# First attention: the values of all nine key tiles of a third of the queries in one group, exponentials in 18 slots, tail keys padded to 128 rows

## The reference, cut to what matters

```python
# _L0_attn_ref: x is (8 images, 1056 tokens, 64), 8 heads of 8 columns
attn = jnp.einsum('bnhd,bmhd->bhnm', q * scale, k)
attn = jax.nn.softmax(attn + bias[None], axis=-1)      # bias depends on n - m
out = jnp.einsum('bhnm,bmhd->bnhd', attn, v).reshape(Bw, Nw, Cd)
```

## Time and profile before

| | |
|---|---|
| median of 3 runs | 2691.78 us (2688.55 to 2697.84) |
| the profiled execution | 2689.29 us, its span 2687.5 us |
| the first attention | from about 335 to 1223 us of the span |
| busy share of the whole span | PE 91%, DVE 71%, ACT 53%, POOL 15% |
| mean granted TensorE clock | 0.91 |

### The profile page before, as it was taken

The page is one execution under the profiler, slowest core; times in us unless marked ns, Lnnn a source line. Parts: engine busy times, 40 slices in busy tenths (PEclk is TensorE's granted clock), DMA queues, the critical chain, the costliest instruction groups (busy, mean ns, idle before and its releaser), DMA issues. The chain is left out here.

```text
span 2687.5 us, 51435 instructions
## 1 busy us (share of the span) xinstructions
PE 2455.1 (91%) x18136; PEld 1069.5 (40%) x18136; DVE 1911.8 (71%) x4910; ACT 1437.0 (53%) x2468; POOL 394.1 (15%) x489
## 2 busy tenths in 40 slices
PE   8987689999999999997799997987799998799999
PEld 3336523333333333335333333666544444433333
DVE  4566688889888889873577776659677774366665
ACT  2117637777777777772344443427666765144333
POOL 2002100000000000005111112132101002311110
PEclk9997779999999999996899999666699999599999
DMA  2114511101010101306100000245612241600110
GB/s 92 24 32 155 194 30 27 37 26 37 25 37 25 37 25 37 61 9 130 28 21 22 22 22 22 65 106 159 226 45 84 64 98 43 138 16 17 32 25 12
DMA packets 233520, 155.14 MB, mean 58 GB/s; under 512 B 187617, under 2 KB 192546, under 8 KB 233042
## 3 DMA queue, kind: packets, MB, share of 16 engines
q1 hardware_dynamic: 220098, 123.57, 17.2%
q0 software_dynamic: 10368, 19.06, 2.5%
q10 hardware_dynamic: 2808, 9.22, 1.5%
HBM read 86.75 MB, written 65.09 MB: 57 GB/s over the span
## 5 line engine op out<-in xcount | busy, mean ns | idle before, releaser
L1666 DVE TENSOR_REDUCE att_mpart<-ps 128x1 f32<-128x512 f32 x1024 | 633.7, 683 | 55.7 <-PE ps L1486 50.6
L1624 ACT ACTIVATE att_p<-ps 128x704 f32<-128x704 f32 x768 | 546.5, 760 | 214.8 <-PE ps L1551 207.8
L1580 PE MATMUL ps<-att_p,att_v 128*9 128x352 f32 x3072 | 300.7, 462 | 0.1
L1486 PE MATMUL ps<-att_kT,att_qT 64*128 64x512 bf16 x1024 | 281.2, 386 | 20.9 <-DMA att_qz<-qt_d 8.4
L1551 PE MATMUL ps<-att_qT,att_kT 64*128 64x352 bf16 x1536 | 251.5, 317 | 7.3 <-ACT att_p L1624 6.9
L1280 DVE TENSOR_REDUCE cau_mpart<-ps 128x1 f32<-128x512 f32 (+5 forms) x384 | 193.1, 552 | 81.1 <-PE ps L1106 61.1
L2418 ACT ACTIVATE mo_act<-ps,mo_b 128x768 f32<-128x768 f32 x176 | 156.3, 901 | 132.0 <-PE ps L2300 127.4
L2571 DVE TENSOR_TENSOR mo_g<-mo_act,ps 128x768 f32<-128x768 f32 x176 | 167.4, 951 | 77.3 <-PE ps L2335 41.2
L1247 ACT ACTIVATE cau_p<-ps 128x704 f32<-128x704 f32 (+6 forms) x272 | 171.6, 660 | 82.3 <-PE ps L1165 49.7
L2970 ACT ACTIVATE mo_act<-ps 128x1024 f32<-128x1024 f32 (+1 forms) x108 | 102.9, 953 | 195.9 <-PE ps L2884 195.6
L1551 PEld LDWEIGHTS ps<-att_qT,att_kT 64*128 64x128 bf16 x1536 | 82.0, 93 | 272.9 <-issue 263.2
(11 more groups left out here) (419 smaller groups left out, 3928.9 us busy)
## 6 DMA issues: line engine op xcount, KB each, us to landing
qt_d<-pre_qT SPq DMA_DIRECT2D x8, 1056.0 KB, 4.3
kt_d<-pre_kT SPq DMA_DIRECT2D x8, 1056.0 KB, 7.3
att_kT<-kt_d SPq DMA_DIRECT2D x32, 264.0 KB, 2.8
att_qT<-qt_d SPq DMA_DIRECT2D x32, 264.0 KB, 3.0
cqt_d<-cpr_qT SPq DMA_DIRECT2D x8, 1056.0 KB
cau_qT<-cqt_d SPq DMA_DIRECT2D x16, 528.0 KB, 4.1
o_d<-att_o POOLq DMA_DIRECT2D x128, 37.1 KB, 2.7
cv_d<-cpr_v POOLq DMA_DIRECT2D x16, 288.0 KB, 6.0
```

What stands on the lines that cost most here:

```text
L1486: mm = pe.matmul(ps[:, bank, :], qT[half(s), u, j * P:(j + 1) * P], kT[half(s), u, c * BANK:(c + 1) * BANK], start=True, stop=not near)
L1580: mm = pe.matmul(ps[32 * cg:32 * cg + DV, 7, 0:TH], v[:, u, i, s, :], p[:, r, s, :], start=i < 2, stop=i == FULL - 1)
L1624: e = act.activation(p[:, n % PRING, :, :], ps[:, bank:bank + 2, 0:TH], ACT.Exp)
L1666: red = dve.tensor_reduce(mpart[:, j, s, c:c + 1], ps[:, bank, :], AX.X, ALU.max)
```

## The change

The nine units of a third become one group, so a third has one `scores` of nine units and one `values` of sixteen matmuls plus two for the tail. `PRING` goes from 4 to 18, two thirds of exponentials. The tail's two value matmuls contract over 128 rows and not 64: `vt` gets 128 rows and POOL sets the lower 64 of `vt` and of the two tail slots of `p` to zero once. In the list of maxima one of the three tail-query maxima moves to index 21, and the order of the last four changes, so that the side steps right ahead of the tail's scores in thirds 0 and 1 are tail-query maxima. The number of side steps behind each unit is a written tuple (`sides`), 13 a third; those of the tail unit come ahead of its scores and not behind. On ACT a finished third is copied out behind the first exponential of the group after the next. Semaphore targets are counted through the whole stage.

```diff
-    QT, MRING, PRING = 2, 3, 4
+    QT, MRING, PRING = 2, 3, 18
...
-    groups = [(t, [(t, i) for i in part]) for t in range(3) for part in ((0, 1), (2, 3), (4, 5), (6, 7), (None,))]
+    groups = [(t, [(t, i) for i in part]) for t in range(3) for part in ((*range(FULL), None),)]
...
-    third_last = [5 * t + 4 for t in range(3)]
+    third_last = list(range(3))
...
-    maxes += [("keys", s, 0, 0) for s in range(2)] + [("query", 0, 0, c) for c in range(3)]
+    maxes.insert(21, ("query", 0, 0, 0))
+    maxes += [("query", 0, 0, c) for c in range(1, 3)] + [("keys", s, 0, 0) for s in range(2)]
...
-    cut = [len(side) * c // NU for c in range(NU + 1)]
+    sides = (2, 1, 2, 1, 1, 2, 1, 1, 2) * 2 + (2, 1, 1, 3, 1, 1, 1, 1, 2)
+    cut = [sum(sides[:c]) for c in range(NU + 1)]
...
-        vt = nm.sb("vt", [64, U, 2, DV])
+        vt = nm.sb("vt", [P, U, 2, DV])
...
+            pool.wait_ge(mz_set, 1)
+            pool.memset(vt[2 * TT:P, :, :, :], 0.0).then_inc(blank, 1)
+            pool.wait_ge(blank, 1)
+            for i in range(2):
+                pool.memset(p[2 * TT:P, NT * i + FULL, :, :], 0.0).then_inc(blank, 1)
+                pool.wait_ge(blank, 2 + i)
...
+                    if i is None:
+                        for pos in range(cut[unit], cut[unit + 1]):
+                            side_step(it, u, pos, last)
+                    at_least(pe, p_made, n - 1)
...
-                    for pos in range(cut[first_unit[g] + c], cut[first_unit[g] + c + 1]):
-                        side_step(it, u, pos, last)
+                    if i is not None:
+                        for pos in range(cut[unit], cut[unit + 1]):
+                            side_step(it, u, pos, last)
...
                     if i is None:
-                        apart(pe, const)
+                        pe.wait_ge(blank, 3)
                     for s in range(2):
                         if i is None:
-                            mm = pe.matmul(ps[64 * s:64 * s + DV, 7, 0:TH], vt[:, u, s, :], p[0:2 * TT, r, 0, :], start=False,
+                            mm = pe.matmul(ps[64 * s:64 * s + DV, 7, 0:TH], vt[:, u, s, :], p[:, r, 0, :], start=False,
                                            stop=True)
...
+                            if c == 0 and len(pending) == 2:
+                                out_third(*pending.pop(0))
+                        pending.append((it, u, t))
```

More of the change, by code:

```diff
@@ L1334, in attend_heads @@
     place = [(m - AHEAD if m >= AHEAD else side.index(("max", 2, m))) % MRING for m in range(NM)]
-    cut = [len(side) * c // NU for c in range(NU + 1)]
+    sides = (2, 1, 2, 1, 1, 2, 1, 1, 2) * 2 + (2, 1, 1, 3, 1, 1, 1, 1, 2)
+    cut = [sum(sides[:c]) for c in range(NU + 1)]
+    assert cut[NU] == len(side) and side[cut[9] - 1][2] == 21 and side[cut[18] - 1][2] == 34
     with ExitStack() as ctx:
@@ L1355, in attend_heads @@
         cdel = nm.sb("cdel", [P, 3, 160 * 8])
-        (set_up, mz_set, mrow_set, t_in, cor_rest, cor_hi, s_mm, p_made, pv_mm, o_cp, mx_mm, mx_red, m_row, m_hi, m_r1, m_mid,
+        (set_up, blank, mz_set, mrow_set, t_in, cor_rest, cor_hi, s_mm, p_made, pv_mm, o_cp, mx_mm, mx_red, m_row, m_hi, m_r1, m_mid,
          c_made, t_mm, t_cp) = nm.sems(
-            "set_up", "mz_set", "mrow_set", "t_in", "cor_rest", "cor_hi", "s_mm", "p_made", "pv_mm", "o_cp", "mx_mm", "mx_red", "m_row",
+            "set_up", "blank", "mz_set", "mrow_set", "t_in", "cor_rest", "cor_hi", "s_mm", "p_made", "pv_mm", "o_cp", "mx_mm", "mx_red", "m_row",
             "m_hi", "m_r1", "m_mid", "c_made", "t_mm", "t_cp")
@@ L1388, in load @@
                              (v[:, u, :, :, :], v_d[bi].rearrange("b p (u t s d) -> (b p) u t s d", u=U, t=NT, s=2)[:, u, :, :, :]),
-                             (vt[:, u, :, :], vt_d[bi].rearrange("b p (h d) -> (b p) h d", d=DV)[:, 2 * u:2 * u + 2, :])):
+                             (vt[0:2 * TT, u, :, :], vt_d[bi].rearrange("b p (h d) -> (b p) h d", d=DV)[:, 2 * u:2 * u + 2, :])):
                 sp.dma_start(dst, src).then_inc(loads[u], 16)
@@ L1541, in scores @@
                 for c, (_, i) in enumerate(parts):
-                    n = u * NU + first_unit[g] + c
-                    pe.wait_ge(p_made, it * U * NU + n - 1 if n >= 2 else it * U * NU)
+                    unit = first_unit[g] + c
+                    n = (it * U + u) * NU + unit
+                    if i is None:
+                        for pos in range(cut[unit], cut[unit + 1]):
+                            side_step(it, u, pos, last)
+                    at_least(pe, p_made, n - 1)
                     apart(pe, const)
@@ L1559, in scores @@
                     mm.then_inc(s_mm, 1)
[L1560 to L1561 removed]
+                    if i is not None:
+                        for pos in range(cut[unit], cut[unit + 1]):
+                            side_step(it, u, pos, last)
             def values(it, u, g):
                 t, parts = groups[g]
[L1566 to L1568 removed]
+                n0 = (it * U + u) * NU + first_unit[g]
+                at_least(pe, o_cp, (it * U + u) * 3 + t)
                 for c, (_, i) in enumerate(parts):
[L1570 removed]
+                    pe.wait_ge(p_made, n0 + c + 1)
                     r = (n0 + c) % PRING
                     if i is None:
[L1573 removed]
+                        pe.wait_ge(blank, 3)
                     for s in range(2):
                         if i is None:
[L1576 removed]
+                            mm = pe.matmul(ps[64 * s:64 * s + DV, 7, 0:TH], vt[:, u, s, :], p[:, r, 0, :], start=False,
                                            stop=True)
@@ L1582, in values, with start @@
                 mm.then_inc(pv_mm, 1)
[L1584 to L1597, removed]
+            def start(k):
+                pe.wait_ge(t_cp, (k + 1) * QT)
+                scores(k // U, k % U, 0, k >= pairs - U)
+            start(0)
+            for k in range(pairs):
+                for g in range(NG):
+                    if g + 1 < NG:
+                        scores(k // U, k % U, g + 1, k >= pairs - U)
+                    elif k + 1 < pairs:
+                        start(k + 1)
+                    values(k // U, k % U, g)
         @block.scalar
@@ L1601, in _, with out_third, step @@
             enter(act, const, "act")
[L1602 to L1609, removed]
+            def out_third(it, u, t):
+                act.wait_ge(pv_mm, (it * U + u) * NG + third_last[t] + 1)
+                if t == 0:
+                    at_least(act, stored[u % 2], (it * (U // 2) + u // 2) * 64)
+                act.activation(o[:, u % 2, t * TH:(t + 1) * TH], ps[:, 7, 0:TH], ACT.Identity).then_inc(o_cp, 1)
+            def step(it, pending):
                 for u in range(U):
@@ L1612, in step @@
                         for c, (_, i) in enumerate(parts):
[L1613 to L1619, removed]
+                            n = (it * U + u) * NU + first_unit[g] + c
+                            act.wait_ge(s_mm, n + 1)
+                            old = n - PRING
+                            if old >= 0:
+                                act.wait_ge(pv_mm, (old // NU) * NG + group_of[old % NU] + 1)
                             bank = 2 * (n % 2)
@@ L1625, in step @@
                             e.then_inc(p_made, 1)
[L1626 to L1633, removed]
+                            if c == 0 and len(pending) == 2:
+                                out_third(*pending.pop(0))
+                        pending.append((it, u, t))
+            pending = []
+            for it in range(IT):
+                step(it, pending)
+            for left in pending:
+                out_third(*left)
         @block.vector
```

## The result

| | before | after |
|---|---|---|
| median | 2690.62 us (2688.55 to 2697.84, 4 runs) | 2965.95 us (2963.68 to 2976.54, 4 runs) |
| ratio after / before | | 1.103 (1.099 to 1.106) |
| the profiled execution, its span | 2689.29 us, 2687.5 us | 2976.54 us, 2974.7 us |
| mean granted TensorE clock of the span | 0.91 | 0.85 |
| one pair of heads, mean over 31 | 26.79 us | 35.05 us |

The kernel is 10% slower. The prediction had 2866 us, with 2930 as the upper end: right in direction, 100 us short. The profiled execution of the changed kernel is the slowest of its four, 10.6 us above their median.

What follows compares the result with a forecast made beforehand. PE was taken to set the pace with 2% to spare, DVE close behind at 11%. Longer pairs (+168), the last pair (+5) and the start (+4) made +177 us on 2689.3: 2866 us, range 2800 to 2930.

Steps and rivals of the forecast that it cites:

- DVE runs dry at the values run: During eighteen value matmuls PE makes no maximum; DVE, with three banks (1.8 us) stored, would idle 2.4 us.
- terms of 6.80 and 3.06: In a third: PE starts side step 13 at 6.80 us, released by DVE; the values run lasts 3.06 us.
- The sum of a pair: First, middle and last third of a pair take 10.6, 10.3 and 11.4 us: 32.3 against 26.8, +5.5.
- 168 forecast: The added 5.5 us a pair, holding for about 30.5 pairs of the stage: +168 us.
- The clock falls: Rival: PE, used less in the DVE-paced phase, drops its clock; 2.9 us more a third, about 3130 us; chance 0.07.
- The other argument: Against a clock fall: where the clock was seen to fall, PE did nothing at all (1660.4 to 1663.8).
- The last pair: Last pair of the stage, paced by ACT: 8.8 us a third against 7.06, +1.7 three times, +5 us.
- The start: At the stage's start the first values come a third later, with the clock lower until then: +4 us.
- The profile I said to look for: In the stage's windows PE's busy share falls to some 80 to 85%, DVE's to about 74%, ACT's to about 60%.
- The sign named as "wrong": Sign against the forecast: a clock under 0.95 in the stage, putting the time above the range.
- 3.4 us a pair of PE's turns: PE's saving from one values group a third instead of five: about 1.1 us a third, 3.4 a pair.

Runs made afterwards that it cites:

- run 4: Changed kernel with each full-maximum reduction on DVE reading 256 of 512 columns, leaving half the keys out of the maxima; 2772.17 us.
- run 5: Changed kernel with full tiles' score matmuls issued twice and full-maximum reductions reading 256 of 512 columns; 2806.33 us.
- run 8: Changed kernel with a third's nine tiles in two groups (0 to 3; 4 to 7 and the tail) instead of one; 2820.80 us.
- run 9: Changed kernel with a third's tiles in four groups, pairs of tiles, the tail with the last pair; 2707.74 us.
- run 10: Kernel of run 9 with a finished third copied out behind the exponentials of the very next group; 2685.86 us.
- run 1: Changed kernel with each full tile's two score matmuls issued twice into the same place (second copies, redundant work); 2885.36 us.
- run 2: Changed kernel with score matmuls issued twice for even key tiles only; 2883.41 us.
- run 3: Changed kernel with score matmuls issued twice for every fourth key tile only; 2900.22 us.
- run 13: Changed kernel with the tail's two value matmuls contracting over 64 rows again, with the turn before them; 2997.96 us.
- run 6: Changed kernel with a third's last three side steps moved behind the first eight value matmuls of the run ahead of it; 2930.59 us.
- run 7: Kernel of run 6 with full tiles' score matmuls also issued twice; 2873.78 us.

## Why the prediction was right or wrong

- **DVE runs dry at the values run: right.** Step 13 at 6.79 us and a values run of 3.17 us (terms of 6.80 and 3.06) stand in the third at the full clock. Half the reductions (runs 4 and 5) take a part of the time away and shorter runs of values (8 to 10) nearly all of it, though these shorten ACT's waits as well as DVE's.
- **The sum of a pair: right at the full clock, to 0.4 us.** 10.6 + 10.3 + 11.4 = 32.3 was forecast; the changed kernel's thirds at 1.00 add up to 31.9. Run 1 has 10.64, 10.47 and 11.47 and a mean of 32.27, 170 us over 31 pairs (168 forecast), but that close a match is partly luck, since its second copies are in it.
- **The clock: the step that failed.** "The clock falls" stood among the rivals at 0.07, "Against it: in the last pair PE was busy 2.65 of 3.4 us and kept 1.00". I took the busy share of a window as the measure. The runs show that it isn't: 78% kept the clock in that row and 85% in run 8, 86% ahead of the fall in the changed kernel did not, and the second copies of run 2 brought it back. (That row has f32 value matmuls among its 24; the new phase has only bf16 ones for 7 us. Whether that is what counts, no run shows.) The other argument, that PE did nothing at all where the clock was seen to fall, rested on one row. The trace of before has, in another stage, a fall under a PE that was busy at the time and for 1.47 of the 2 us ahead (a wait of 1.99 us lies further back), and 28 us at 0.50 with PE counted busy throughout:

```profile
1708.00:1710.00 2.00, 1.47 (x18) 1.29 (x18) 2.00 (x7) 0.61 (x2) 0.00 (x0) 1.00 0.40 93
1710.00:1712.00 2.00, 2.00 (x12) 1.37 (x11) 2.00 (x9) 1.61 (x4) 0.00 (x0) 0.59 0.23 50
...
1772.00:1800.00 28.00, 28.00 (x196) 23.50 (x194) 15.01 (x67) 4.40 (x13) 11.52 (x13) 0.50 0.64 142
```

The fall costs 2.8 us a pair by run 1 and 3.1 by the thirds at 1.00, so 86 to 97 us over 31 pairs: most of the shortfall of 100. The rival's own 3130 was too high, since the clock comes back within the values run (4.76 us and not 6) and four of nine thirds keep it.
- **The last pair: mis-sized.** From the last turned add to the last copy out it took 1499.6 - 1455.6 = 44.0 us, before 1222.7 - 1196.9 = 25.8: +18, where I had +5. These rows of PE in the changed kernel show the part that I left out:

```profile
1490.79 4.44 PE L1593 MATMUL ps<-att_p,att_v 128*9 128x352 f32 x32
1495.06 0.76 PE L1589 MATMUL ps<-att_p,att_vt 128*9 128x352 f32 x4
1496.39 2.56 PE L1593 MATMUL ps<-att_p,att_v 128*9 128x352 f32 x32 [0.57 <-ACT att_o L1618]
1498.76 0.76 PE L1589 MATMUL ps<-att_p,att_vt 128*9 128x352 f32 x4
```

The values of the last third stand alone behind those of the third before, with no scores to hide them, and the clock fell here as well. In run 1, with the clock at 0.96 there, the same stretch took 1408.5 - 1369.6 = 38.9. So about 5 of the 13 us too few are the clock's.
- **The start: not settled.** The 4 us forecast were for the first values coming a third later at the lower clock. The first turned add came 2.6 us later (369.0, before 366.4), but it stands ahead of all values, and at that place the runs that share its code up to there differ as much (364.2 in run 3, 369.2 in run 1).
- **The account.** 8.26 x 31 = 256, 18 and 2.6 make 277 of the 287 us by which the span grew. The other 10 lie behind the stage (1475.1 us from the last copy to the end, 1464.8 before). They are not the change's: no edit touches what runs there, and the same stretch took 1475.8 us in run 1, 1463.1 in run 9 and 1466.6 in run 13.
- **The profile I said to look for.** PE's busy share did not fall "to some 80 to 85%" (it is 89%), in part because the lower clock stretches what counts as busy: the four thirds at 1.00 stand at 83 to 89%. The sign named as "wrong" was the right one: "a clock under 0.95 in the stage, which would put the time above my range".

The Trainium skill, TensorE: Matmul & The Clock Gate, section "A second HAM failure mode: psum-queue depth-cycling", tells of a kernel whose TensorE idled for moments between groups of matmuls as it cycled through PSUM banks, and whose clock swung between its two levels. This trace agrees in kind: PE's waits for DVE and ACT in the changed phase are at most 0.6 us long, the clock between 0.50 and 1.00. Run 8 has waits of the same kind (up to 0.5 us, 157 of them) and kept 1.00, so they alone do not decide it.

What stays open: which property of PE's work decides the clock; the second copies both fill gaps and add columns, and no run parted the two. Why run 10, which has a turn less a third than the kernel before, gains 0.2 us a pair and not the 0.8 that three turns of 0.28 would be. What holds the thirds of runs 5 and 7 (10.0 and 10.7 us), ACT or PE or their waits for each other. And run 4's remaining falls.

## What to carry to other kernels

A run of matmuls that feeds no consumer should be shorter than what each consumer has stored: here three banks held 1.8 us for DVE and two double banks two exponentials, about 1.4 us, for ACT, and a run of 3.1 us starved both; putting maxima into its midst (runs 6 and 7) won little. Merging groups was to save 3.4 us a pair of PE's turns (an estimate) and made the pair 5.1 to 5.5 us longer, 8.3 with the clock; pad or align shapes first, and merge only up to the stored work. When a change makes the busiest engine wait in small pieces, read the granted clock stretch by stretch, and test it by giving TensorE redundant matmuls: if the time falls and the clock comes back, the clock was a part of the loss.

## What the runs showed of the hardware

- The granted clock fell to 0.50 in the midst of a stage in which PE was busy 89% of the time, though PE's waits for other engines were at most 0.6 us long (500 to 1100) and it was busy for 3.49 of the 4.08 us ahead of one such fall, and it did so in a pattern of nine thirds that repeated through the stage.
- Redundant matmuls made a kernel 81 us faster: 2965.95 to 2885.36 us with two more matmuls per full unit, and 2900.22 with a quarter of them.
- At 2.4 GHz a run of eighteen f32 value matmuls (352 columns, four column strips) took 3.17 us; entered at 1.2 GHz it took 4.76, since the clock came back on its way, and 5.70 in the last pair (1479.05 to 1484.75), where it came back only near the end.
- In the kernel before, from 1772 to 1800, PE was counted busy for all of 28 us while the granted clock stayed at 0.50.
